# Attention scores: the causal mask is written into PSUM ahead of the score products

## What is computed

```
kqv = layernorm(x) @ Wqkv + bqkv            # 16 heads of 32
scores = einsum('bsnh,btnh->bnst', k, q) / sqrt(32)
scores = triu(scores) + -10000.0 * tril(ones, k=-1)
attn = softmax(scores, axis=2)              # scores of the masked triangle vanish
out = einsum('bnkq,bknh->bqnh', attn, v) ... @ Wo + bo
```

## Time and profile before

| | |
|---|---|
| median of 3 runs | 3175.32 us |
| range of the runs | 3170.45 to 3177.17 us |
| the profiled execution | 3185.54 us, span 3183.8 us |
| mean granted TensorE clock | 0.977 |
| PE matmul busy | 3000.3 us (94%) |
| PE weight load busy | 2059.9 us (65%) |
| DVE busy | 2082.6 us (65%) |
| ACT busy | 1118.9 us (35%) |
| score products L839, L859 | 233.6 and 264.1 us, 768 each |
| mask products L842, L862 | 120.0 and 116.3 us, 512 each |

### The profile page before, as it was taken

One profiled execution on the slowest core, in us unless ns is written; L12 is line 12 of the kernel. 1 busy time (PEld: TensorE's weight loads), 2 busy tenths in 40 slices (PEclk: granted clock), 3 DMA queues, 4 the chain that ended last, 5 costly groups with the idle time before them and its releaser, 6 DMA issues.

```text
span 3183.8 us, 59539 instructions
## 1 busy us (share of the span) xinstructions
PE 3000.3 (94%) x20836; PEld 2059.9 (65%) x20836; DVE 2082.6 (65%) x2942; ACT 1118.9 (35%) x1749; POOL 751.9 (24%) x1061
## 2 busy tenths in 40 slices
PE   3899999999899999999989999999998999999998
PEld 3555467777665447777765545877775554677776
DVE  2566664777756665677766666477776666647777
ACT  2133334444223323444322332444421333244442
POOL 3211102333221101333312110133321211023332
PEclk7899999999999999999999999999999999999999
DMA  9322111111222202111132320211123222021112
GB/s 340 84 47 66 27 44 47 52 44 45 91 47 67 66 21 54 46 43 52 41 94 47 73 47 14 67 43 51 40 68 86 49 46 47 23 69 47 49 45 77
DMA packets 163747, 191.57 MB, mean 60 GB/s; under 512 B 43962, under 2 KB 103994, under 8 KB 161786
## 3 DMA queue, kind: packets, MB, share of 16 engines
q1 hardware_dynamic: 157150, 175.83, 20.3%
q10 hardware_dynamic: 6432, 13.63, 1.4%
HBM read 106.99 MB, written 23.36 MB: 41 GB/s over the span
## 4 chain that ended last, share of the span: by engine, by line
PE 76%; DVE 9%; SPq 4%; issue 4%; DMA 4%; ACT 1%; POOL 1%; ACTq 0%; DVEq 0%; POOLq 0%
PE ps L724 14%; PE ps L725 13%; PE ps L726 13%; PE ps L876 7%; PE ps L839 5%; PE ps L859 5%; PE ps L1069 4%; PE ps L953 3%; PE ps L1055 2%; DMA KS<-EV 2%; PE ps L1115 2%; PE ps L1078 2%; DVE mneg L1575 1%; SPq L463 1%; PE ps L734 1%
## 5 line engine op out<-in xcount | busy, mean ns | idle before, releaser
L724 PE MATMUL ps<-uh,win 128*128 128x512 f32 x1536 | 629.7, 410 | 11.6 <-POOL win L1818 10.9
L725 PE MATMUL ps<-ul,win 128*128 128x512 f32 x1536 | 603.1, 393 | 0.0
L726 PE MATMUL ps<-uh,win 128*128 128x512 f32 x1536 | 602.7, 392 | 0.0
L1575 DVE TENSOR_REDUCE mneg<-ps 128x1 f32<-128x128 f32 (+7 forms) x512 | 361.6, 752 | 140.2 <-PE ps L842 137.7
L1252 ACT ACTIVATE PR<-ps 128x1024 f32<-128x1024 f32 (+3 forms) x384 | 310.0, 809 | 394.9 <-PE ps L862 253.6
L724 PEld LDWEIGHTS ps<-uh,win 128*128 128x128 f32 x1536 | 290.3, 189 | 105.9 <-issue 29.6
L876 PE MATMUL ps<-PR,VG 128*32 128x512 f32 (+3 forms) x1536 | 329.5, 504 | 12.7 <-DVE OS L1581 8.3
L726 PEld LDWEIGHTS ps<-uh,win 128*128 128x128 f32 x1536 | 289.7, 189 | 65.4
L878 PE MATMUL ps<-PR,ones 128*32 128x512 f32 (+3 forms) x1536 | 329.4, 504 | 0.0
L1687 DVE TENSOR_TENSOR LM<-ps,LM 128x512 f32<-128x512 f32 x256 | 170.2, 686 | 242.4 <-PE ps L1069 198.6
L725 PEld LDWEIGHTS ps<-ul,win 128*128 128x128 f32 x1536 | 290.7, 189 | 53.6
(11 more groups left out here) (221 smaller groups left out, 5029.2 us busy)
## 6 DMA issues: line engine op xcount, KB each, us to landing
raw<-in_t SPq DMA_DIRECT2D x128, 256.0 KB, 2.7
QS<-EV SPq DMA_DIRECT2D x192, 128.0 KB, 2.5
KS<-EV SPq DMA_DIRECT2D x168, 128.0 KB, 2.5
in_t<-tiles ACTq DMA_DIRECT2D x10, 1024.0 KB, 9.6
XN<-in_L_attn_a_x_dram SPq DMA_DIRECT2D x40, 256.0 KB, 5.6
win_raw<-in_L_attn_a_Wqkv_dram SPq DMA_DIRECT2D x34, 256.0 KB, 3.4
win_raw<-in_t SPq DMA_DIRECT2D x32, 256.0 KB, 2.7
edec<-ed_t SPq DMA_DIRECT2D x512, 16.0 KB, 1.5
```

The source lines that it names most:

```text
L724: pe.matmul(dst, hi_l, hi_r, start=first, stop=False)
L725: pe.matmul(dst, hi_l, lo_r, start=False, stop=False)
L726: return pe.matmul(dst, lo_l, hi_r, start=False, stop=last)
L1575: dve.tensor_reduce(mneg[:, hh, t:t + 1], wide(b0)[:, 0:(t + 1) * P], AX.X, ALU.max, negate=True).then_inc(a_max.sem, 1)
```

## The change

In pass A the mask matmul is issued ahead of the score products of its tile, opens the accumulation (`start=True`) and the last score product, which covers the diagonal, is added onto it (`start=False`). In pass B the masks of both heads are issued first, then the two score products, which are added onto them. The number of instructions, their operands and all waits stay; the semaphore that tells of a finished tile is now on a score product. `keep_awake` with its four products stays at both places.

```diff
@@ scores_a
                     b0 = MAX_BANK[t]
                     n = (t + 1) * P
+                    at = t * P % HB
+                    pe.matmul(ps[:, b0 + t * P // HB, at:at + P], identb[:, :], mask_ts[:, :], start=True, stop=False, skip_group_check=True)
                     for c in range(0, n, HB):
                         m = min(HB, n - c)
-                        diag = c + m == n
                         i = pe.matmul(ps[:, b0 + c // HB, 0:m], QS[slot][0:STACK, hh, t * P:(t + 1) * P],
-                                      KS[slot][0:STACK, hh, c:c + m], start=True, stop=not diag)
-                        if diag:
-                            i = pe.matmul(ps[:, b0 + c // HB, m - P:m], identb[:, :], mask_ts[:, :], start=False, stop=True)
+                                      KS[slot][0:STACK, hh, c:c + m], start=c + m < n, stop=True, skip_group_check=True)
                     i.then_inc(a_pe.sem, 1)
@@ scores_b
                     diag = s * P >= c * HB
+                    if diag:
+                        for hh in range(2):
+                            pe.matmul(ps[:, SCORE_BANK[u] + hh, 0:P], identb[:, :], mask_st[:, :], start=True, stop=False, skip_group_check=True)
                     for hh in range(2):
                         i = pe.matmul(ps[:, SCORE_BANK[u] + hh, 0:n], KS[slot][:, hh, s * P:(s + 1) * P],
-                                      QS[slot][:, hh, t0:t0 + n], start=True, stop=not diag)
-                        if diag:
-                            i = pe.matmul(ps[:, SCORE_BANK[u] + hh, 0:P], identb[:, :], mask_st[:, :], start=False, stop=True)
+                                      QS[slot][:, hh, t0:t0 + n], start=not diag, stop=True, skip_group_check=True)
                     i.then_inc(st_pe.sem, 1)
```

## The result

| | before | after |
|---|---|---|
| median, 7 runs each | 3177.81 us (3170.45 to 3187.01) | 3159.61 us (3156.39 to 3165.12) |
| ratio, 95% interval | | 0.994 (0.9924 to 0.9956) |
| profiled execution, its span | 3185.5, 3183.8 us | 3160.7, 3158.9 us |
| mean granted clock | 0.977 | 0.979 |

The change makes the kernel about 18 us faster, by the ratio 14 to 24. Forecast were 3158 us and a saving of 17.4. The sum is right to a few us; one of its terms is wrong, and the others make up for it.

The account below looks back on a forecast made before the run. TensorE, busy 94% of the span, was taken as the bound, its savings worth full price except before waits. Per-pair savings of 14.4 us plus 3.0 made 17.4, from the 3175.3 median to 3158 us; 8-in-10 range 3149 to 3175.

Parts of the forecast that it names:

- the rival in which the switch of type costs: Both passes: switching between fp32r and bf16 costs, so only waits move, 3175 us; shares chance 0.12 with the order-worth-nothing rival.
- the one in which order is worth nothing: Both passes: the switch or each load by itself costs, whatever the order; 3175 us, chance 0.12.
- a drain there: Pass B: a mask behind a mask takes 0.17 us, not 0.06, leaving nothing of 17.4; 3175 us, chance 0.07.
- A unit behind a projection: Pass B: first load hidden either way, one uncovered load before and after; saving 0.
- The `hf == 1` pairs lose what they save ahead of step 2: Units 0, 2, 3: unit 0 saves nothing, the others' saving turns into longer waits for the stacking DMAs.
- The rival in which it falls: Waits at step 2 lengthen past 0.99 to 2.04 us and the clock drops: 3194 us, slower, chance 0.07.
- 3.0 us ahead of step 2: Units 0, 2, 3 in 11 `hf == 0` pairs of groups 1 to 3 save 0.27 each, data being mostly there; bound below 0.
- A masked unit behind a drain: Pass B behind `weigh`: exposed load falls from 0.10 to 0.01 us, saving 0.09, or 0.04 with 128 columns.
- The uncovered load: Product first behind a mask: its fp32r weight load, which the short mask doesn't cover, taken as 0.05 us.
- one sign of being wrong: Pass B: the prediction is wrong if the first product behind the masks takes 0.10 us more than its columns.
- The maxima were to swallow the saving at the end of a pair: `hf == 1` pairs: savings between step 7 and transposed maxima are swallowed by 0.55 us issue and 1.23 us reduction.
- The rival in which more is swallowed: DMAs take the 3.0 us ahead of step 2, VectorE 6.2 in pairs without projections; 8 us left, 3167, chance 0.08.

Follow-up runs that it names:

- mask_f32r: Changed kernel with identity and masks in fp32r instead of bf16, same order: 3188.69 us against 3180.76 before, ratio 1.0029.
- b_alternate: Changed kernel, but pass B issues mask, product, mask, product: 3159.05 us against 3179.98 before, ratio 0.9933.
- no_awake: Changed kernel without the four unread products ahead of pass A at step 2 of `hf == 1` pairs: 3187.79 us against 3180.76 before, ratio 1.0025.
- undo_first: Changed kernel with units 0 to 3 of pass B back in the old order: 3157.01 us against 3180.76 before, ratio 0.9917.
- Half and half: Kernel before with only pass B changed: 3175.43 us, ratio 0.9984; with only pass A changed: 3159.46 us, ratio 0.9935; both against 3179.98.
- pass A alone: Kernel before with only pass A changed, pass B as before: 3159.46 us against 3179.98, ratio 0.9935.
- the freer pairs: Changed kernel with pass A's tiles paired only where both banks are free early (0 with 1, 2 with 3): 3154.77 us against 3180.63 before, ratio 0.9912.
- awake_first: Changed kernel with four more unread products at step 2 of each sequence's first pair: 3156.58 us against 3180.63 before, ratio 0.992.
- both: Changed kernel with the first-pair unread products and pass A's free tile pairs together: 3156.06 us against 3180.63 before, ratio 0.9914.
- before_awake: Kernel before with four more unread products at step 2 of each sequence's first pair: 3178.94 us against 3182.14 before, ratio 0.9995.

## Why the prediction was right

**The mechanism holds.** `mask_f32r` rules out the rival in which the switch of type costs; `b_alternate` (0.81 us beside 0.87 and 0.74 for the same work) rules out the one in which order is worth nothing; the 0.06 between masks rules out a drain there. That a load overlaps only when row groups differ, the rule of the Trainium skill in "TensorE: Matmul & The Clock Gate", Part 3, The mechanism, would have made all orders equal. The loads here share their rows (96 or 97 of the products, 128 of the masks), and the kernel with the long load in front is 29 us slower than the one with the short one. The measurement decides against the rule for this kernel. The same section of the Trainium skill also names a background weight buffer, for which a load is pulled ahead of running matmuls; the prediction read only the rule, and the hidden loads here (0.24 against 0.34 us for like products) agree with the buffer.

**Steps that came out as forecast.** The masks stand 0.06 apart, and a product starts 0.03 or 0.04 behind its mask. A unit behind a projection gains nothing or next to it: 0.76 before (from 1077.70 in the earlier trace rows to `weigh` at 1078.46), 0.74 after (988.71 to 989.45). The `hf == 1` pairs lose what they save ahead of step 2. The clock stayed. The rival in which it falls, the one on the slower side, had its condition right: it wanted waits longer than 0.99 us, they came to 0.56, and `no_awake` shows the price once they pass to 1.7.

**The term that was wrong: 3.0 us ahead of step 2.** I took the data to be there in the `hf == 0` pairs, because PE mostly did not wait. They came just in time instead. PE arrived earlier and 8 new waits appeared, of 0.2 to 0.5 us. The stretches ahead of the first tile, first pairs aside, add up to 276.2 us before and 276.1 after: 0.2 us of the 3.0, and they lie in group 3. `undo_first` shows the same from the other side. "No wait" in a profile means that the slack is at least zero, not how much there is. I had written that I could not see it, kept 0 as the other bound, and then took the full value; the row does not speak for that.

**The terms that were too small.** A masked unit behind a drain was to save 0.09 and saves 0.13 (0.87 to 0.74). From start to start its parts were 0.34, 0.04, 0.32 and 0.17 before and are 0.06, 0.03, 0.32 and 0.33 after. Three differences make up the 0.13. The first load is the largest: the product that led the unit took 0.11 more than the 0.23 of a product behind a product, and the leading mask takes its columns and nothing more. The prediction had 0.10 less 0.01. The load behind two masks (0.06 less its columns, 0.03 and 0.32) is some 0.01 shorter than behind one (0.04 and 0.32), and the end of the unit, the drain ahead of `weigh`, comes out at 0.10 either way, to 0.01 (0.33 less 0.23 behind a product, 0.17 or 0.16 less 0.06 behind a mask).

The uncovered load was too small as well: 0.05, where mask and product take 0.36, of which 0.23 and 0.06 are columns and 0.07 is left; `b_alternate` measured the same 0.07. Where the number of such loads changes (the units of 128 columns, the tiles that VectorE waits for) the term follows it. This is also why one sign of being wrong all but came true: the product behind the masks was to be followed 0.23 later, and 0.10 more was to mean an error. It takes 0.32, 0.09 more. But that is what a product behind a mask took before, too (1142.44 to 1142.76 in the earlier trace rows); the forecast of 0.23 overlooked the uncovered load that its own sum has there, and that load stands in both orders. From the rows of before, 0.06 + 0.04 + 0.32 + 0.32 (the last from an unmasked unit, 1144.45 to 1144.77) would have given the 0.74. By pair, predicted and measured on the path:

| | predicted | measured | per sequence |
|---|---|---|---|
| `hf == 0` with projections, from step 2 | 0.49 | 0.69 | 3 |
| `hf == 1`, from step 2 | 0.39 | 0.53 | 3 |
| group 3, `hf == 0`, from step 2 | 0.39 | 0.53 | 1 |
| last pair | 0.58 | 0.74 | 1 |
| units 0, 2, 3 ahead of step 2, `hf == 0`, 11 in the kernel | 0.27 | 0.14 in group 3, none in groups 1 and 2 | 2.75 |

The measured values are means over the four sequences. Outside the first pairs I predicted 17.4 less 4 x 0.49 = 15.4 us and measured 17.1. The wrong 3.0 was made good by savings a quarter to two fifths larger than forecast. That the sum came out is luck in this part. So is the closeness of 3158 to 3159.61: it was reckoned from 3175.3, the median of three runs of before, and seven give 3177.81. A right total is no proof of its terms.

**What the waits took back.** The maxima were to swallow the saving at the end of a pair; that wait grew 7.8 to 10.1 us and the outputs' 8.3 to 10.2. The rival in which more is swallowed (8 us left) fell all the same: of its two parts the first came true, while VectorE, busy 19.23 of the 24.66 us of a pair without projections, did not set the pace.

**What stays open.** Half and half give 4.6 and 20.5 us, the whole 18: by the stretches they overlap, by the medians pass A alone does it all. The intervals reach 5 to 7 us each way, so the split rests on the stretches. Why the unread products at the first pair and the freer pairs don't add up is settled in part only: in `awake_first` and `both` PE waits 0.75 us on average at the first tile of the third pair of a sequence, where it waits 0.39 after, so a part of what the first pair gains is lost in the next `hf == 0` pair.

## What to carry to other kernels

In a stream of matmuls count the stretches between drains, and let each begin with the shortest weight load: a short accumulating matmul (here the mask) costs no more first than last, and in front its load exposed nothing where the long one exposed 0.11 us. Group such short matmuls so that only one long load stands behind them, but never let the group ask for a buffer earlier than the single instruction did. Before you count a saving that lies ahead of a transfer, find out by how much the transfer is early; where PE doesn't wait now, it may the moment it is faster.

## What the runs showed of the chip

- The clock fell to 1.2 GHz (granted 0.50) behind idle times of only 1.67 to 1.71 us, in 9 of 12 places of like kind, and stayed there for stretches such as the 6.4 us above. Behind waits of 0.5 to 0.6 us after four unread products it held. Those products, 1.2 us of useless work each time, are worth 28 us by the medians.
- In the first pair of a sequence the clock fell in some sequences and not in others, without any difference in the program: 32.2 to 39.8 us for the same work within one execution of before. Four such pairs can spread the time of a run by more than most edits here are worth.
- `before_awake` shows that the kernel before gained nothing in its median (ratio 0.9995) from a first pair that never lost its clock in its profiled execution, though the four of them went from 147.7 to 132.8 us there. In that execution 3.4 us came back in the other stretches (809.6 to 813.0): the first tile of the third pair waited 0.54 to 0.78 us for the stacking DMAs, where it had not waited. Where the rest was lost in the medians was not found.
- A product with `start=False` that covers up to 512 columns, of which the mask had written 128, left right scores in all of them: it was added onto the mask on those 128 columns and not onto the older contents of the others.
